# The router of tiles 1 to 3 as split products and packed logits, with five output products ahead of the second base block

## The reference

```python
def _L0_cond_ref(x, language_ids, W, Wr, A, B):
    base = jnp.einsum('btd,od->bto', x, W)
    logits = jnp.einsum('btd,ed->bte', x, Wr)
    bias = jax.nn.one_hot(tgt, E) * LANG_BIAS
    logits = logits + bias[:, None, :]
    topw, topi = jax.lax.top_k(logits, TOP_K)
    weights = jax.nn.softmax(topw, axis=-1)
    gates = jnp.sum(jax.nn.one_hot(topi, E) * weights[..., None], axis=-2)
    h = jnp.einsum('btd,erd->bter', x, A)
    lora_out = jnp.einsum('bter,bte,eor->bto', h, gates, B)
    return base + SCALING * lora_out
...
def _L1_cond_ref(x, A, B, adapter_ids):
    Bx = jnp.einsum('bni,bri->bnr', x, B[adapter_ids])
    return jnp.einsum('bnr,bor->bno', Bx, A[adapter_ids]) * SCALING
...
x = x + _L0_cond_ref(x, itok_B_0_7, L0_W, L0_Wr, L0_A, L0_B)
x = x + _L1_cond_ref(x, L1_A, L1_B, itok_B_4_50)
```

## Time and profile before

| | us |
|---|---|
| median of 3 runs | 97.96 |
| lowest, highest | 97.57, 98.14 |
| the profiled execution | 98.09 |
| its span, first to last instruction | 96.2 |
| TensorE busy | 91.3 |
| DVE, ACT, POOL busy | 60.4, 43.8, 36.6 |

### The profile page before, as it was taken

The page is one execution under the profiler, slowest core; times in us unless marked ns, Lnnn a source line. Parts: engine busy times, 40 slices in busy tenths (PEclk is TensorE's granted clock), DMA queues, the critical chain, the costliest instruction groups (busy, mean ns, idle before and its releaser), DMA issues.

```text
span 96.2 us, 2162 instructions
## 1 busy us (share of the span) xinstructions
PE 91.3 (95%) x733; PEld 77.5 (81%) x733; DVE 60.4 (63%) x215; ACT 43.8 (46%) x88; POOL 36.6 (38%) x44
## 2 busy tenths in 40 slices
PE   4999999999999999999999999999999999999940
PEld 1499888889888897889888888889888888998940
DVE  4249799220699469860299379860399289863960
ACT  2570556629939960298028950497038500001100
POOL 5000767999521099991000099950000540000000
PEclk9999999999999999999999999999999999999996
DMA  1997987863915322798322224997000005050084
GB/s 21 363 325 194 329 328 174 266 174 66 354 58 131 76 49 65 201 374 218 72 48 50 46 57 127 383 238 286 9 0 3 7 0 214 4 218 0 7 267 169
DMA packets 14843, 14.36 MB, mean 149 GB/s; under 512 B 9968, under 2 KB 11248, under 8 KB 14448
## 3 DMA queue, kind: packets, MB, share of 16 engines
q1 hardware_dynamic: 13904, 11.85, 38.4%
q0 software_dynamic: 640, 2.10, 7.8%
q10 hardware_dynamic: 288, 0.28, 1.1%
HBM read 10.02 MB, written 4.19 MB: 148 GB/s over the span
## 4 chain that ended last, share of the span: by engine, by line
PE 92%; DVE 3%; DVEq 0%; issue 0%
PE main L653 15%; PE main L659 15%; PE main L665 15%; PE aw_ps L695 14%; PE side L747 6%; PE main L680 4%; PE main L679 4%; PE main L681 4%; PE aw_ps L771 3%; PE main L794 3%; PE side L695 3%; DVE xs L543 3%; PE side L727 2%; PE main L771 1%; PE side L771 1%; PE aw_ps L653 1%
## 5 line engine op out<-in xcount | busy, mean ns | idle before, releaser
L330 POOL TENSOR_TENSOR x_lo<-xs,x_hi 128x512 fp32r<-128x512 f32 x12 | 15.2, 1295 | 16.1 <-ACT x_hi L351 16.0
L653 PE MATMUL main<-x_hi,w_hi 128*128 128x512 f32 (+1 forms) x64 | 17.6, 397 | 0.0
L659 PE MATMUL main<-x_hi,w_lo 128*128 128x512 f32 (+1 forms) x64 | 16.9, 385 | 0.0
L665 PE MATMUL main<-x_lo,w_hi 128*128 128x512 f32 (+1 forms) x64 | 16.8, 384 | 0.0
L695 PE MATMUL aw_ps<-aws,xs 128*128 128x136 f32 x112 | 14.6, 284 | 0.0
L695 PEld LDWEIGHTS aw_ps<-aws,xs 128*128 128x128 f32 x112 | 14.2, 195 | 0.2
L659 PEld LDWEIGHTS main<-x_hi,w_lo 128*128 128x128 f32 x64 | 11.8, 188 | 2.6
L665 PEld LDWEIGHTS main<-x_lo,w_hi 128*128 128x128 f32 x64 | 11.8, 188 | 2.4
L653 PEld LDWEIGHTS main<-x_hi,w_hi 128*128 128x128 f32 x64 | 11.3, 188 | 2.2
L383 ACT ACTIVATE a_ops<-a_hi 64x512 fp32r<-64x512 f32 x12 | 7.6, 630 | 11.6 <-POOL a_rest L298 11.5
L502 DVE TENSOR_TENSOR xs<-main,xs 128x512 f32<-128x512 f32 x15 | 9.9, 684 | 2.1 <-PE main L681 2.1
(11 more groups left out here) (107 smaller groups left out, 134.8 us busy)
## 6 DMA issues: line engine op xcount, KB each, us to landing
out_t<-xs SPq DMA_DIRECT2D x16, 256.0 KB
xs<-x_t SPq DMA_DIRECT2D x3, 1024.0 KB, 4.7
b1s<-b_t SPq DMA_DIRECT2D x64, 32.0 KB, 1.9
xs<-x_t SPq DMA_DIRECT2D x4, 256.0 KB, 4.1
ws<-w_t SPq DMA_DIRECT2D x4, 256.0 KB, 4.8
b0s<-b_t SPq DMA_DIRECT2D x1, 256.0 KB, 5.2
aws<-aw_t ACTq DMA_DIRECT2D x1, 204.0 KB, 4.0
rows<-a_t,row_at POOLq DMA_INDIRECT x8, 3.9
```

The costliest lines, as they stand in the source:

```text
L330: nc.gpsimd.tensor_tensor(x_lo[:, t % 2, c], xs[:, t, c], x_hi[:, t % 2, c].bitcast(F32), ALU.subtract).then_inc(x_lo_ready, 1)
L653: nc.tensor.matmul(out_ap, w_hi[:, c, k], x_hi[:, s, k, n], start=(k == 0), stop=False)
L659: nc.tensor.matmul(out_ap, w_lo[:, c, k], x_hi[:, s, k, n], start=False, stop=False)
L665: last = nc.tensor.matmul(out_ap, w_hi[:, c, k], x_lo[:, s, k, n], start=False, stop=False)
```

## The change

For tiles 1 to 3 the router is taken apart. The logits become a block of their own, `logits_product(u)`: the 32 last columns of the router weights are the stationary operand and x streams, four token quarters side by side in the array, so that experts lie on the partitions; DVE adds the bias and turns 32x32 blocks (`block_logits`). It stands behind the down block of tile u-2 (for u = 1 ahead of tile 0's transposes). h becomes `h_product(u)`, twelve fp32r products of 128x512 from x_hi, x_lo and the router weights split into aw_hi and aw_lo, with ranks on the partitions at once, so that the transposes of tiles 1 to 3 fall away. The gates then have to lie along the tokens and repeat over the ranks: DVE turns the gates (gate_t), SP writes them to DRAM, waits, and reads them back spread over 128 partitions (gate_rows, `spread_gates`), and DVE multiplies h by them in PSUM (`gate_h_t`). ACT and DVE then split h there into gt_hi and gt_lo.

Five of a tile's output products move from behind base(t+1, 1) to ahead of it, and the banks of up_banks change. SP's and POOL's orders are written anew: x of tile 2 is issued between the first two groups of b1 loads, x of tile 3 behind the fourth, the gate transfers between them, and the stores of tiles 0 and 1 earlier. Tile 0 keeps its router. The diff, cut to its core:

```diff
+        aw_hi, aw_lo = sb("aw_hi", [P, K, H], F32R), sb("aw_lo", [P, K, H], F32R)
...
+        gate_t = sb("gate_t", [P, NB - 1, CW])
+        gate_rows = sb("gate_rows", [P, NB - 1, TB])
+        gate_dram = nc.dram_tensor("gate_rows_t", (NB - 1, experts, TB), F32, kind="Internal").ap()
...
-        up_banks = main[2:] + side[:1] + aw_ps + side[:1] + aw_ps
+        h_bank, logits_bank = aw_ps
+        up_banks = main[2:] + side + [logits_bank, h_bank] + side
...
+            def spread_gates(u):
+                sp.wait_ge(gate_t_ready, u)
+                sp.dma_start(gate_dram[u - 1].rearrange("e (q i) -> q e i", i=CW), gate_t[:, u - 1])\
+                  .then_inc(gate_written, 16)
+                sp.wait_ge(gate_written, 16 * u)
+                sp.dma_start(gate_rows[:, u - 1], gate_dram[u - 1].unsqueeze(1).broadcast_to([experts, rank, TB]))\
+                  .then_inc(gate_spread[u], 16)
+            def store(t):
                 for c in range(K):
                     sp.wait_ge(x2_ready, t * PARTS + (c + 1) * GPB)
                     sp.dma_start(out[:, t, c, :], xs[:, t, c, :]).then_inc(stored, 16)
+            sp.wait_ge(clamped_ready, 1)
+            load_b1(0)
+            sp.dma_start(xs[:, 2], x[:, 2]).then_inc(x_loaded[2], 16)
+            load_b1(1)
+            spread_gates(1)
+            sp.wait_ge(down_done, GPB)
+            load_b1(2)
+            load_b1(3)
+            sp.dma_start(xs[:, 3], x[:, 3]).then_inc(x_loaded[3], 16)
+            spread_gates(2)
+            load_b1(4)
+            load_b1(5)
+            store(0)
+            spread_gates(3)
+            load_b1(6)
+            load_b1(7)
+            store(1)
+            store(2)
...
+            def x_rest(t, c):
+                pool.wait_ge(x_hi_ready, t * K + c + 1)
+                if t >= 2 and c == 0:
+                    pool.wait_ge(base_done, (t - 1) * K)
+                nc.gpsimd.tensor_tensor(x_lo[:, t % 2, c], xs[:, t, c], x_hi[:, t % 2, c].bitcast(F32),
+                                        ALU.subtract).then_inc(x_lo_ready, 1)
+            pool.wait_ge(aw_lo_ready, 1)
+            x_rest(1, 0)
+            x_rest(1, 1)
+            split_a1(0)
+            split_a1(1)
+            x_rest(1, 2)
+            x_rest(1, 3)
+            pool.wait_ge(down_done, GPB)
+            gather(SLOTS)
+            for t in range(2, NB):
+                pool.wait_ge(gate_t_ready, t)
                 for g in range((t - 1) * GPB, t * GPB):
-                    if t > 1:
-                        split_a1(g)
-                    if g >= 1 and g - 1 + SLOTS < NG:
+                    split_a1(g)
+                for c in range(K):
+                    x_rest(t, c)
+                for g in range((t - 1) * GPB, t * GPB):
+                    if g - 1 + SLOTS < NG:
                         gather(g - 1 + SLOTS)
+            for g in range((NB - 1) * GPB, NG):
+                split_a1(g)
...
+                    act.wait_ge(gated_t_ready, u)
                     act.wait_ge(lora_done, u * K)
-                round_hi(gt_hi[:], side[1][:], gt_hi_ready)
+                    round_hi(gt_hi[:], h_bank[:], gt_hi_ready)
...
+            act.wait_ge(aw_loaded[1], 16)
+            round_hi(aw_hi[:], aws[:, :, 0:H], aw_hi_ready)
...
+            def block_logits(u):
+                dve.wait_ge(logits_done, u)
+                nc.vector.scalar_tensor_tensor(
+                    logits_t[:], is_block_language[:, u - 1].unsqueeze(2).broadcast_to([P, TILES, CW]), LANG_BIAS,
+                    logits_bank[:, 0:P].rearrange("p (b i) -> p b i", b=TILES), ALU.mult, ALU.add)\
+                    .then_inc(logits_taken, 1)
+                dve.wait_ge(logits_taken, u)
+                then_wait(nc.vector.transpose(logits_b[:], logits_t[:]))
...
+                    nc.vector.transpose(gate_t[:, u - 1], gate[:].rearrange("p b e -> p (b e)")).then_inc(
+                        gate_t_ready, 1)
...
+            def gate_h_t(u):
+                dve.wait_ge(h_done, u)
+                dve.wait_ge(gate_spread[u], 16)
+                nc.vector.tensor_tensor(h_bank[:], h_bank[:], gate_rows[:, u - 1], ALU.mult).then_inc(gated_t_ready, 1)
...
+                    if t == 0:
+                        gates(1)
+                    if t + 2 < NB:
+                        block_logits(t + 2)
+                        top_two(logit_b)
+                        pick(logit_b)
                     for g in range(t * GPB, (t + 1) * GPB):
                         down_rest(g)
+                    gate_h_t(t + 1)
                     gt_rest(t + 1)
+                    if t + 2 < NB:
+                        gates(t + 2)
...
+            def logits_product(u):
+                pe.wait_ge(x_loaded[u], 16)
+                if u == 1:
+                    pe.wait_ge(gated_ready, 2)
+                elif u == 2:
+                    pe.wait_ge(logits_taken, 1)
+                else:
+                    pe.wait_ge(x2_ready, (u - 3) * PARTS + up_banks.index(logits_bank) + 1)
+                for k in range(K):
                     for j in range(TILES):
-                        last = aw_product(0, j, k)
-                last.then_inc(aw_done, 1)
-            def aw_tiles(u):
-                pe.wait_ge(x_loaded[u], 16)
-                pe.wait_ge(gated_ready, u * 2)
-                if u >= 2:
-                    pe.wait_ge(x2_ready, (u - 1) * PARTS)
-                for j in range(TILES):
-                    for k in range(K):
-                        last = aw_product(u, j, k)
-                last.then_inc(aw_done, 1)
-            def gt_transposes(u):
-                pe.wait_ge(gated_ready, u * 2 + 1)
-                if u == 0:
-                    pe.wait_ge(const_ready, 3)
+                        last = nc.tensor.matmul(logits_bank[j * CW:(j + 1) * CW, 0:P], aws[:, k, AWN - CW:AWN],
+                                                xs[:, u, k, j * P:(j + 1) * P], start=(k == 0), stop=(k == K - 1),
+                                                tile_position=(0, j * CW))
+                last.then_inc(logits_done, 1)
+            def h_product(u):
+                s = u % 2
+                pe.wait_ge(aw_hi_ready, 1)
+                pe.wait_ge(aw_lo_ready, 1)
+                if u == 1:
+                    pe.wait_ge(gated_ready, 2)
                 else:
-                    pe.wait_ge(down_ready, u * GPB)
+                    pe.wait_ge(x2_ready, (u - 2) * PARTS + up_banks.index(h_bank) + 1)
+                for k in range(K):
+                    nc.tensor.matmul(h_bank[:], aw_hi[:, k], x_hi[:, s, k], start=(k == 0), stop=False)
+                for k in range(K):
+                    nc.tensor.matmul(h_bank[:], aw_lo[:, k], x_hi[:, s, k], start=False, stop=False)
+                for k in range(K):
+                    last = nc.tensor.matmul(h_bank[:], aw_hi[:, k], x_lo[:, s, k], start=False, stop=(k == K - 1))
+                last.then_inc(h_done, 1)
...
+            logits_product(1)
+            gt_transposes()
...
+                    logits_product(t + 2)
                 base(t + 1, 0)
-                gt_transposes(t + 1)
-                base(t + 1, 1)
+                h_product(t + 1)
                 for i in range(EARLY):
                     up(t, i)
+                base(t + 1, 1)
```

More of the change, by code:

```diff
@@ L171, in two_block_kernel @@
         gap_ready, gated_ready = sem("gap_ready"), sem("gated_ready")
+        aw_hi_ready, aw_lo_ready = sem("aw_hi_ready"), sem("aw_lo_ready")
+        logits_done, logits_taken = sem("logits_done"), sem("logits_taken")
+        h_done, gated_t_ready, gate_t_ready = sem("h_done"), sem("gated_t_ready"), sem("gate_t_ready")
+        gate_written = sem("gate_written")
+        gate_spread = [None] + [sem(f"gate_spread{u}") for u in range(1, NB)]
         x2_ready, row_at_ready, clamped_ready = sem("x2_ready"), sem("row_at_ready"), sem("clamped_ready")
@@ L194, in packed, with h_parts @@
             return g // GPB < NB - 1
-        def h_parts(u):
-            if u == 0:
-                banks, n = [side[1], side[0]] + aw_ps, 1
-            else:
-                banks, n = aw_ps, TILES // 2
-            return [(slice(i * n, (i + 1) * n), bank[:, 0:n * AWN].rearrange("p (j n) -> p j n", j=n))
-                    for i, bank in enumerate(banks)]
+        def h_parts():
+            return [(j, bank[:, 0:AWN]) for j, bank in enumerate([side[1], side[0]] + aw_ps)]
         block = ctx.enter_context(nc.Block())
@@ L537, in gt_rest @@
                 dve.wait_ge(gt_hi_ready, u + 1)
-                split_lo(gt_lo[:], side[1][:], gt_hi[:], gt_lo_ready)
+                if u >= 1:
+                    dve.wait_ge(lora_done, u * K)
+                split_lo(gt_lo[:], (h_bank if u else side[1])[:], gt_hi[:], gt_lo_ready)
             def add_x2_last(s, c):
@@ L606, in _ @@
                         add_x2(t - 1, range(EARLY, PARTS))
-                    if c == (K - 1 if t else 1) and more:
-                        top_two(t + 1)
```

(19 more changed lines are left out.)

144 lines of the change are left out of this document (75 added, 69 removed).

## The result

| | before | changed |
|---|---|---|
| median, us | 97.81 (97.48 to 98.14) | 99.81 (98.93 to 101.32) |
| profiled execution, us (its span) | 98.09 (96.2) | 99.70 (98.0) |
| TensorE, first product to end of the last, us | 91.34 | 93.43 |

The changed kernel takes 1.0174 times the time of the kernel before, 95% interval 1.0124 to 1.0224. The medians are of six runs each; the ratio leaves out the changed kernel's two slow runs, 100.65 and 101.32, and so stands for 1.7 us where the medians differ by 2.00. TensorE's own stretch grew by 2.09 us. The profiled pair differs by 1.6, since what lies behind TensorE's last product was 0.3 shorter in the changed kernel's execution, and what lies around the span 0.2. So the whole answer lies in TensorE's stretch.

A forecast was written before the change was run, and what follows sets the result against it. The kernel was taken as bound by TensorE, 92% of the chain of waits. -12.45 + 8.31 + 1.86 + 2.23 = -0.05 us, so 98.04 on the profiled scale, 97.9 as a median; range 96.8 to 99.0.

The forecast's parts named there:

- What TensorE gives up: Tiles 1 to 3: three router blocks at 3.71 us and three transpose groups at 0.44 go, 12.45 us saved.
- What TensorE gets: Three h blocks, 8.31 us in all, and logits blocks of 0.93 each, the second and third adding 1.86.
- rival (c): Logits products don't run side by side: 3.5 us a block, +6.4, 104.4 us; chance 0.06.
- SP's queue in tile 0: Tile 2's x load delays the second b1 group to 25.3, so tile 0's down block waits: +2.23 us (1.5 to 2.9).
- Rival (a): No wait at tile 0's down block, b1 group in by 24.1: -1.18 us, median 96.8; chance 0.20.
- The gate's way through DRAM: Tile 0: gate arrives E + 6.1 to 8.3, middle 6.8 (E: down block's end on TensorE); no wait until E + 7.3.
- rival (b): Gates' round trip late in tile 0, TensorE waits before third base block or first lora: up to +1.0, median 98.9; chance 0.16.
- What was costed at nothing: Router weight split on ACT and DVE, POOL's later x_lo, SP's later tile 3 x load, stores: all covered, 0 us.
- The output products ahead: Output products ahead of the second base block: the same products, no cost, letting the gate arrive as late as E + 7.3.
- The range: Whole kernel's median: 96.8 to 99.0 us, from the middle of rival (a) to the upper end of rival (b).
- The sign named for being wrong in kind: An idle of TensorE in tiles 2 or 3, or logits blocks of over 2 us.
- tile 0's term: Tile 0's down block: +2.23 us, about 1.1 the first logits block with two changes of kind, the rest a new wait.

The follow-up runs named there:

- the later gates: VectorE makes the gates of the tile after next behind the first pair of output additions, against the changed kernel: 100.57 us, 1.0265 times the kernel before.
- 46.86 to 50.09 above: Trace of the changed kernel with tile 2's x load ahead of both b1 groups and gates behind the first output additions: 99.62 us, ratio 1.0123.
- x of tile 2 first: Changed kernel with the load of x of tile 2 ahead of both groups of b1 loads: 98.27 us, 1.0022 times the kernel before.

## Why the prediction was wrong

The prediction was 97.9 with no change as the likeliest case; the time is 99.81, above its range. Three steps failed: the price of what TensorE gives up, the gate's read, and above all POOL's gathers, which were costed at nothing without a reason. By its own steps, with what each adds to the sum:

*What TensorE gives up* was counted too high. The pieces of the chain, 3.71 and 0.44, hold the change of kind ahead of the block behind them, which stays when the block goes. From start to start it was 3.61 and 0.36: 11.9 in all, not 12.45. The text said that both prices hold it, and took them whole. +0.5.

*What TensorE gets* was right: h blocks 2.79 against 2.77; logits blocks 1.01 from start to start, 0.08 above the 0.93 from the fours of the down block and below the 1.14 estimated from the Trainium skill (TensorE: Matmul & The Clock Gate, Part 3: Packing small matmuls). They do run side by side, so rival (c) is out. +0.2.

*SP's queue in tile 0* was right in mechanism, and in size for the profiled execution: x of tile 2 at 24.06 (23.3 to 24.1 was given), the b1 group at 25.68 (25.2 to 26.0), one idle of 1.02 (1.1). Rival (a) is out. The step had the widest range in the text and came out best, because it was built from landings of this kernel. That the size agrees to 0.1 is in part luck: the same idle was 0.97 and 0.53 in two other traces.

*The gate's way through DRAM* failed, at the read. The gate left VectorE at 28.60, E + 1.8 (2.2 given), and the write took 1.96 (1.9). The middle of the text left 2.7 for the read. It took 4.46, above both bounds, 1.9 and 4.1; in the experiments with 8 rows it took 3.7 to 4.4 from issue to use, at the upper bound rather than the middle. The bounds are loads whose outermost dimension is 128 partitions, and this one has 8 rows outermost and gets half the engines: 256 KB at 204 and not 369 GB/s are some 0.6 us more. The rest of the excess in this execution isn't explained by any row. The gate arrived at 35.06, E + 8.3, the upper end of rival (b), and the chain behind it took 4.6 as worked out (35.15 to 39.74). So (b) came true with its place, its releaser and nearly its price, 0.75 of idle against 1.0. By the section of the Trainium skill that the prediction cited (DMA: Bandwidth & Descriptors, Anatomy of one DMA), an estimated 2.6 for the read, it would have been no wait; this trace disagrees. That section is on transfers that GpSimd issues, and its formula has no term for the number of engines; the rule on that number stands elsewhere on the same page of the Trainium skill, and the prediction didn't use it. +0.8.

*What was costed at nothing* failed at POOL. The text follows POOL's splits and x_lo (it gave their end as E + 17.7; it was 46.14, E + 19.4, early enough) and stops there. The diff also moves two gathers past the four x_lo, to 46.28 and 47.54, beside tile 1's down block. No term, no rival and no bound had them. The rule that every instruction of a moved step counts, on every queue, was not followed to POOL's last two instructions. +0.7.

*The output products ahead* were costed at nothing, and that held.

*The range* ended at (b)'s upper end, 99.0, which holds both waits, tile 0's and the gate's. With them alone the kernel would have been inside. What lies above is in no case of the text: the saving that was counted 0.5 too high, the pause of 0.7, and the start, 0.2. Together: -0.05 + 0.5 + 0.2 - 0.2 (tile 0's term, 2.03 against 2.23) + 0.8 + 0.7 + 0.2 (start) = 2.15, against 2.09 on TensorE; the experiments removed the two waits and the pause one by one. The sign named for being wrong in kind, an idle in tiles 2 or 3, did not show; the idle that no step had came in tile 1.

## What to carry to other kernels

When a chain is one engine from end to end, a change that takes work from it must be followed on every other queue to the last instruction that it moves: here 0.5 us of saved work were lost several times over to a load in the wrong place, a read on half the engines and two gathers beside a dense block. Look at the outermost dimension of both sides of a DMA (8 rows got half the engines here, 16 all of them), and issue gathers while the matrix engine runs long products, not while it runs many short ones. An edit that removes a wait can move another engine's work onto something else (the later gates cost 0.8 us until the gathers were put elsewhere, and then gave 0.45), so look at the whole tile again after each.

## What the hardware showed

- Gathers issued by POOL beside a block of 32 or 64 small products (64 or 128 columns of data each) can stop TensorE for 0.3 to 0.6 us at a time, between products without a wait: once in the changed kernel, three times in 46.86 to 50.09 above, and in the kernel before as soon as its gathers were put there (down block 3.04 us for 1.34). The same gathers beside long products (40.30 and 42.75 before), or with only their data moving beside the down block, did nothing. Single gathers at 16.76 (1.32 us, beside the first logits block from 17.23) and 27.18 did nothing either, so not every meeting costs; where the line is was not tried.
- A read of 256 KB with 8 source rows moves at 204 GB/s on half the engines, with 16 rows at 369 GB/s on all.
- Small loads behind a 1 MB load on one queue wait for it: 2.7 to 4.9 us to landing for eight b1 loads that took 1.6 to 2.8 in the kernel before, and 1.9 to 3.0 with x of tile 2 first.
